# Selectors of the aggregations made in three pieces between the sums into G

## What is computed

```
def _rel_graph_conv(h, src, dst, etypes, norm, basis, comp, bias, loop_w, apply_relu):
    hb = jnp.einsum('nd,bdo->bno', h, basis)
    coef = comp[etypes]
    m = coef[:, 0, None] * hb[0][src]
    for b in range(1, basis.shape[0]):
        m = m + coef[:, b, None] * hb[b][src]
    m = m * norm[:, None]
    agg = jax.ops.segment_sum(m, dst, num_segments=n)
    out = agg + bias + h @ loop_w
...
x = _layernorm(x + _L0_gnn_ref(...))   # the above twice, 4 bases, 8 relations
x = _layernorm(x + _L1_gnn_ref(...))   # 8 bases, 32 relations
x = _layernorm(x + _L2_gnn_ref(...))   # mean over neighbours, two dense products
x = _layernorm(x + _L3_gnn_ref(...))   # 4 blocks of 4-head attention over edges and an MLP
```

## Time and profile before

| what | value |
|---|---|
| time, median of 3 runs | 3223.38 us |
| the profiled execution, from its first to its last instruction | 3335.5 us |
| PE busy in it | 3088.8 us (93%) |
| DVE busy | 2098.9 us (63%) |
| ACT busy | 1382.5 us (41%) |
| POOL busy | 1351.8 us (41%) |
| the sums into G, L969 | 663 of them, 454.2 us |
| the selector matmuls, L846 | 1326 records (2 for each), 701.7 us |

### The profile page before, as it was taken

The page is one execution under the profiler, slowest core; times in us unless marked ns, Lnnn a source line. Parts: engine busy times, 40 slices in busy tenths (PEclk is TensorE's granted clock), DMA queues, the critical chain, the costliest instruction groups (busy, mean ns, idle before and its releaser), DMA issues.

```text
span 3335.5 us, 42860 instructions
## 1 busy us (share of the span) xinstructions
PE 3088.8 (93%) x14927; PEld 2211.3 (66%) x14948; DVE 2098.9 (63%) x4788; ACT 1382.5 (41%) x2130; POOL 1351.8 (41%) x1097
## 2 busy tenths in 40 slices
PE   6999997988977787899999999999999999999999
PEld 3333675433762224687645899879987899879987
DVE  7999423776345664425536777667777667767767
ACT  6888632000332002334225455435554345425554
POOL 4777336666347775443211211341025212251023
PEclk8999998999998888999999999999999999999999
DMA  3666524666324443322401200130011300140012
GB/s 98 177 178 177 193 79 127 177 181 179 101 85 136 127 124 101 103 94 72 154 13 39 89 14 30 61 109 14 8 61 44 102 14 29 48 123 14 8 61 76
DMA packets 138459, 301.39 MB, mean 90 GB/s; under 512 B 29981, under 2 KB 47709, under 8 KB 137218
## 3 DMA queue, kind: packets, MB, share of 16 engines
q0 software_dynamic: 53040, 154.26, 16.6%
q1 hardware_dynamic: 83762, 141.72, 13.4%
q10 hardware_dynamic: 1440, 2.62, 0.2%
HBM read 269.51 MB, written 27.46 MB: 89 GB/s over the span
## 4 chain that ended last, share of the span: by engine, by line
PE 81%; DVE 9%; issue 4%; DMA 2%; ACT 2%; another core or an unknown queue 1%; POOL 1%; SPq 0%; DVEq 0%; POOLq 0%; ACTq 0%
PE bank L846 17%; PE bank L153 15%; PE bank L155 14%; PE bank L154 14%; PE bank L2446 5%; PE bank L856 3%; PE bank L2110 3%; PE bank L1752 2%; PE bank L823 2%; DVE G L969 2%; DVE y_tile L2062 1%; DVE y_tile L2064 1%; DVE x_stats L2045 1%; DMA yT_lo<-yT_new_lo 1%; PE bank L1026 1%
## 5 line engine op out<-in xcount | busy, mean ns | idle before, releaser
L846 PE MATMUL bank<-gathered,selector 128*128 128x512 f32 x1326 | 701.7, 646 | 134.8 <-DVE G L969 62.3
L969 DVE TENSOR_TENSOR G<-G,bank 128x512 f32 x663 | 454.2, 685 | 305.5 <-PE bank L846 211.8
L846 PEld LDWEIGHTS bank<-gathered,selector 128*128 128x128 f32 x1326 | 231.2, 202 | 438.2 <-issue 407.1
L833 ACT COPY G<-bank 128x512 f32<-128x512 f32 x160 | 82.3, 653 | 637.1 <-remote 287.8
L2534 ACT CAST probT<-bank 128x512 fp32r<-128x512 f32 (+2 forms) x480 | 212.2, 515 | 263.0 <-PE bank L2446 262.1
L1424 POOL TENSOR_TENSOR weight_parts<-weight_ring,weight_parts 128x512 fp32r<-128x512 f32 x130 | 187.4, 1442 | 299.3 <-ACT weight_parts L1357 299.2
L872 ACT ACTIVATE sign_src<-node_iota_16bit,src_float 128x1251 bf16<-128x1251 f16 x208 | 276.6, 1340 | 56.2 <-PE bank L856 29.2
L2616 DVE CUSTOM_DVE_ANT_0 prob<-bank,count_by_src 128x512 f32<-128x512 f32 (+1 forms) x480 | 258.4, 589 | 58.8 <-PE bank L155 58.8
L788 POOL DMA_INDIRECT gathered<-x_rows,src_index x236 | 238.7, 1012 | 120.7 <-issue 58.1
L2542 DVE TENSOR_TENSOR probT<-bank,probT 128x512 fp32r<-128x512 f32 (+2 forms) x480 | 254.2, 585 | 51.9 <-ACT probT L2534 51.2
L1383 DVE TENSOR_TENSOR lhs_parts<-G,lhs_parts 128x640 fp32r<-128x640 f32 x122 | 101.8, 835 | 292.0 <-ACT lhs_parts L1355 291.9
(11 more groups left out here) (292 smaller groups left out, 7062.1 us busy)
## 6 DMA issues: line engine op xcount, KB each, us to landing
weight_ring<-in_L_gnn_basis SPq DMA_DIRECT2D x64, 256.0 KB, 2.7
weight_ring<-in_L_gnn_bases SPq DMA_DIRECT2D x64, 256.0 KB, 2.6
x_L<-x_rows SPq DMA_DIRECT2D x50, 256.0 KB, 4.5
x_rows<-x_L SPq DMA_DIRECT2D x50, 256.0 KB, 5.5
yT_hi<-yT_new_hi SPq DMA_DIRECT2D x4, 2560.0 KB, 10.9
yT_lo<-yT_new_lo SPq DMA_DIRECT2D x4, 2560.0 KB
count_rows<-count SPq DMA_DIRECT2D x10, 640.0 KB, 5.9
count_by_dst<-count_rows SPq DMA_DIRECT2D x10, 640.0 KB, 9.3
```

The costliest lines, as they stand in the source:

```text
L846: pe.matmul(bank[s % banks][:], sel[:, s % SELECTORS, :], xs[:, s % slots, :], start=True, stop=True).then_inc(*multiplied.inc())
L969: dve.tensor_tensor(g, g, bank[s % banks][:], ALU.add).then_inc(*added.inc())
```

## The change

`select(i)` is split into `mask(i)`, which makes `same` for a batch of 4, and `fill(first)`, which makes the selectors of PAIR = 2 steps (128 x 256 elements). `select_beside(s)` puts them behind the sums: the mask of batch i + 2 behind sum 0 of batch i, a fill behind sum 1, and a fill behind sum 2. In L0a they stand ahead of that step's `count_add`. PE now waits for selectors in every second step. The first two batches are still made ahead of the loop, in six instructions where there were four. Nothing is changed on ACT, POOL and SP.

```
+PAIR = 2
...
         for s in range(steps):
             pe.wait_ge(*gathered[s % slots](s // slots + 1))
-            if s % BATCH == 0:
-                pe.wait_ge(*selected(s // BATCH + 1))
+            if s % PAIR == 0:
+                pe.wait_ge(*selected(s // PAIR + 1))
...
-    def select(i):
+    def mask(i):
 
         first, n = i * BATCH, min(BATCH, steps - i * BATCH)
-        if first >= SELECTORS:
-            dve.wait_ge(*multiplied(first - SELECTORS + n))
         if i:
-            dve.wait_ge(*selected(i))
+            dve.wait_ge(*selected(first // PAIR))
         dve.tensor_tensor(
             same[:, 0:n, :],
...
+    def fill(first):
+
+        n, at, i = min(PAIR, steps - first), first % SELECTORS, first // BATCH
+        if first >= SELECTORS:
+            dve.wait_ge(*multiplied(first - SELECTORS + n))
         dve.wait_ge(*compared(i + 1))
-        at = first % SELECTORS
         dve.tensor_tensor(
             sel[:, at:at + n, :].rearrange("p t (b n) -> p t b n", b=nb),
...
+    def select_beside(s):
+
+        i, at = s // BATCH + 2, s % BATCH
+        if at == 0 and i < batches:
+            mask(i)
+        first = i * BATCH + PAIR * (at - 1)
+        if 0 < at <= BATCH // PAIR and first < steps:
+            fill(first)
...
-                if s // BATCH + 2 < batches:
-                    select(s // BATCH + 2)
...
             dve.tensor_tensor(g, g, bank[s % banks][:], ALU.add).then_inc(*added.inc())
+            select_beside(s)
             if counting:
                 c, m = divmod(s, PATHC.tiles)
```

More of the change, by code:

```diff
@@ L905, in select @@
             ALU.is_equal).then_inc(*compared.inc())
+    def fill(first):
+        n, at, i = min(PAIR, steps - first), first % SELECTORS, first // BATCH
+        if first >= SELECTORS:
+            dve.wait_ge(*multiplied(first - SELECTORS + n))
         dve.wait_ge(*compared(i + 1))
-        at = first % SELECTORS
         dve.tensor_tensor(
             sel[:, at:at + n, :].rearrange("p t (b n) -> p t b n", b=nb),
-            same[:, 0:n, :].rearrange("p t (b n) -> p t b n", b=1).to_broadcast([P, n, nb, path.nodes]),
+            same[:, first % BATCH:first % BATCH + n, :].rearrange("p t (b n) -> p t b n", b=1).to_broadcast(
+                [P, n, nb, path.nodes]),
             co[:, :, first:first + n].rearrange("p (b n) t -> p t b n", n=1).to_broadcast([P, n, nb, path.nodes]),
             ALU.mult).then_inc(*selected.inc())
+    def select_beside(s):
[5 more added lines that the diff above has]
+            fill(first)
     def windows_of(p, first, n):
@@ L942, in on_dve @@
             dve.wait_ge(*laid(1))
-        select(0)
-        select(1)
+        for i in range(2):
+            mask(i)
+            for first in range(i * BATCH, (i + 1) * BATCH, PAIR):
+                fill(first)
         if counting:
```

## The result

The changed kernel takes 3256.0 us (median of 4 runs, 3252.5 to 3257.7), the kernel before 3223.2 us in the runs beside it (4 runs, 3220.2 to 3223.6). The ratio is 1.0107, with a 95% interval of 1.0092 to 1.0121. So it is slower by 34 us (30 to 39). Forecast was 3251 us.

What follows compares the result with a forecast made beforehand. The prediction took a loop through PE and DVE to bound L0a, and mostly POOL to pace L0b and L1. Fills at +33 us and relief at -5 us gave +28 us, so 3251 us, with an 8-in-10 range of 3218 to 3282.

Steps and rivals of the forecast that it cites:

- The loop in L0a: L0a: a batch is a loop through PE and DVE, growing from 5.79 to 6.46 us by two fills.
- DVE's wait ahead of sum 1: L0a after the change: DVE would wait for PE some 0.7 us there in each batch.
- The 0.14 us a batch: L0a before the change: the rest between the 5.79 us loop and the 5.93 us batch, taken as scatter.
- The fill at 0.33 us: L0a, DVE: each 128x256 fill adds 0.33 us start to start, with bounds of 0.30 and 0.60 us.
- The size: L0a: fills behind the sums of 50 batches, 100 x 0.33 us, cost +33 us.
- L0b and L1 at -5 us: L0b and L1: POOL mostly sets the pace, so relief on DVE brings -5 us, between 0 and -20.
- the count of 41 batches: L0b and L1: 19 + 22 batches at DVE's pace, each 0.50 us shorter, bounding the relief at 20 us.
- The span of the changed kernel's profile: Whole kernel: 3348 to 3364 us, from the earlier profiled 3335.5 us with +33 and up to -20.
- A: L0b and L1: the relief is real outside the profile, -20 instead of -5 us, total 3236 us; chance 0.17.
- C: L0a: PE loses its clock once less busy, +47 us with a clock as in L1, total 3298 us; chance 0.08.
- B: L0a: PE alone bounds it and the change removes hold-ups, -17 us, total 3186 to 3201 us; chance 0.12.
- D: Whole kernel: fills at +30 us and relief of -25 to -30 cancel, within 7 us of before; chance 0.07.

Runs made afterwards that it cites:

- e5: Changed kernel, but in L0a the mask and both fills stand behind sum 0: 3224.8 us against 3220.2 before the change, ratio 1.0017.
- e6: Changed kernel with the three count_adds behind sums 0, 1 and 2 instead of 1, 2 and 3: 3214.9 us, ratio 0.9984 to the kernel before.
- e12: Changed kernel, unedited, on the fourth chip: 3352.2 us against 3326.1 for the kernel before, ratio 1.0085.
- e10: Kernel before the change with count_adds behind sums 0, 1 and 2, on the fourth chip: 3326.3 us against 3326.1, ratio 0.9999.
- e11: Changed kernel with count_adds behind sums 0 to 2 and the mask behind sum 3, fourth chip: 3318.0 us against 3326.1 before the change, ratio 0.9984.
- e4: Kernel before the change, unedited, run again for a second profile: 3223.2 us, ratio 1.0000, profile span 3223.5 us.
- e3: Kernel before, but in L0a the mask stands behind sum 0 and the whole selector, one 128x512 instruction, behind sum 1: 3257.5 us, ratio 1.0108.
- e2: Kernel before with the three pieces in L0b and L1 alone, L0a as before: 3220.7 us, ratio 0.9997.
- e7: Changed kernel with all three pieces and also the one-hot behind sum 0 in L0a: 3223.9 us, ratio 1.0011 to the kernel before.

## Why the prediction was right

- **The loop in L0a.** Right. Sum 1 to 2 was forecast at 2.13 and is 2.17 us (of this the one-hot takes 0.64 instead of 0.60 us in the batch shown), 2 to 3 1.53 and 1.53, 3 to 0 0.90 and 0.90. The part that should stay, sum 3 to sum 1, was forecast at 2.80 us and is 2.79. Only one sign was worked out wrongly: DVE's wait ahead of sum 1 was put at some 0.7 us. The forecast's own terms give 2.80 - 0.90 - 0.60 - 0.30 = 1.00, and it is 1.01. PE's busy share is 89%, not 87%. e5 and e6 show it from two sides: moving the pieces back into DVE's wait, or taking the third count_add off the loop, removes the loss, and e12 with e10 and e11 shows it on another chip. The 0.14 us a batch that the prediction calls scatter were 13 long batches of 45 in the first profile. In e4 there are 3, and the mean is 5.80.
- **The fill at 0.33 us.** Right (204.11 to 204.44). It lasts 0.42 us. By this the trace agrees with the Trainium skill, VectorE: DVE Perf Modes, section on the TRN2 errata, whose formula gives 424 ns for 256 columns. Its advice against small tiles is true here by 0.06 to 0.09 us a batch (e3), about a tenth of the loss.
- **The size.** +33 us forecast, +34 measured in L0a (50 x 0.69). The ratio of the kernels is 1.0107 instead of 1.0086.
- **L0b and L1 at -5 us.** The sign was right, the size small enough not to matter: -3.3 us by the stages, -1 us (-4 to +2) in e2. The reason was false, so that the term came out near is luck. I had fitted 117 us of POOL's waits to 112 us between the profiled and the other runs. e4 shows that the 112 us are the chip's, and that POOL waits for PE for 18.0 and 6.7 us in the ordinary case, so it doesn't run through either. Nor do batches at DVE's pace turn into time where PE is held up (e12). Batches of 3.66 us do occur as forecast, 6 in L0b and 7 in L1 of the changed kernel. But the count of 41 batches from the earlier trace rows is a count of waits, and no measure of what DVE costs: in e4 18 batches take the 4.16 to 4.23 us of DVE's pace, and L0b and L1 together became only 3.3 us shorter.
- **The span of the changed kernel's profile.** Forecast 3348 to 3364, is 3254.6 us, since it came from an ordinary chip. On a chip of the other sort it spans 3349.6 us (e12). A forecast against a profiled execution holds only for its chip.
- **The rivals.** A (relief of 20 us) is false by e2, C by the clock of 1.00 with PE at 89%: the pauses in which PE waited for DVE, 0.69 us a batch, didn't lower it, and in e12 it is 0.99. The 0.97 and 0.83 of the earlier trace rows on which C rested are those of the slower sort of chip; in e4 L0b and L1 are at 1.00. The Trainium skill, TensorE: Matmul & The Clock Gate, warns in its section on the second HAM failure mode of small idles between groups; L0a at 1.00 doesn't show it. B (PE alone bounds L0a) is false for before, though the chain with 97% on PE would have it, and nearly true for e6 (5.69 us a batch against PE's own 5.60). D is false, as nothing was there to cancel.

## What to carry to other kernels

Where two engines hand work to and fro through a small ring, the chain of waits may put all of it on one of them; walk one period on both timelines, and mark where each engine waits. Work that can be moved is free in the wait of its engine, up to the wait's length, and costs its full start-to-start time in the part without a pause: the same three instructions cost 3 us behind sum 0 and 34 us spread behind three sums. Once the wait is full, another chain can set the pace, and shortening the first one further brings nothing (e7). Here it was better to take the instruction that closes the loop one step earlier than to move work round it (e6; on the slower sort of chip the total didn't gain by it). Before a number of a profile is explained, compare its span with the median of the runs, and take a second profile where they differ.

## What the runs showed of the hardware

- The same kernel took 3220 to 3223 us on two chips and 3326 to 3347 us on two others, on one core, with a mean granted clock of 0.988 and 0.97. By stage, with the clock in the third column from the right, of e12 for L0b and L1 (L0a is at 0.99):

```profile
580.00:890.00 310.00, 269.97 (x813) 126.35 (x813) 204.24 (x398) 17.33 (x33) 195.65 (x203) 0.94 0.61 173
1020.00:1400.00 380.00, 297.12 (x778) 126.38 (x779) 212.40 (x431) 60.62 (x71) 248.59 (x247) 0.88 0.44 119
```

  and of e4, for L0b and L1:

```profile
542.00:807.00 265.00, 254.72 (x814) 120.12 (x812) 206.43 (x346) 16.44 (x32) 196.26 (x204) 1.00 0.71 203
942.00:1273.00 331.00, 284.39 (x780) 110.83 (x778) 214.61 (x366) 54.92 (x73) 244.65 (x243) 1.00 0.49 135
```

  The ordinary chip keeps 1.00 in both, where the clock here falls to 0.94 and 0.88. L0a differs least: 0.99 in e12 and in e4 (45 to 348 us). The cause is open.
- From a mask to the first fill behind it on the same engine, which waits for it on a semaphore, it takes 0.43 and 0.39 us (e5, e7), though the mask itself lasts 0.28 to 0.33 us. Before the change the same pair took 0.31 us. One thing in the program differs: there the wait for old matmuls stood ahead of the mask, here it stands between mask and fill. Whether that is the reason was not tested.
